# Out projection of a head pair as seven block products of a 2 by 2 scheme, summed in four PSUM banks, on one Trainium2 core

## The reference

```
q = layernorm(x) @ Wq; k, v = ctx @ Wk, ctx @ Wv
attn = softmax(q k^T / sqrt(128)) per head           (256 x 256)
x = x + concat_heads(attn @ v) @ Wo                  (2048 -> 512)
h = layernorm(x); top-4 of 32 experts from sigmoid(h @ gate_w.T) + bias, 2 of 4 groups, capacity 1024
out = x + sum of the chosen experts' silu(h w1) * (h w3) @ w2, weighted
        + silu(h @ shared_gate) * (h @ shared_up) @ shared_down
```

## Time and profile before

| | |
|---|---|
| median of 3 runs | 1640.73 us (1638.84 to 1643.18) |
| profiled execution, its own time | 1646.64 us |
| profiled execution, span | 1644.9 us |
| TensorE (PE) busy | 1605.2 us, 98% |
| VectorE (DVE) busy | 1215.0 us, 74% |
| ScalarE (ACT) busy | 844.8 us, 51% |
| GpSimdE (POOL) busy | 793.6 us, 48% |

### The profile page before, as it was taken

The page is one execution under the profiler, slowest core; times in us unless marked ns, Lnnn a source line. Parts: engine busy times, 40 slices in busy tenths (PEclk is TensorE's granted clock), DMA queues, the critical chain, the costliest instruction groups (busy, mean ns, idle before and its releaser), DMA issues. The chain is left out here.

```text
span 1644.9 us, 35029 instructions
## 1 busy us (share of the span) xinstructions
PE 1605.2 (98%) x12199; PEld 1147.0 (70%) x12199; DVE 1215.0 (74%) x3524; ACT 844.8 (51%) x2094; POOL 793.6 (48%) x1088
## 2 busy tenths in 40 slices
PE   8999999999999999999999999999999999999995
PEld 5667677777777777777777677777777666666663
DVE  7988787777778787787778787877766266776762
ACT  6764444454454454454545454454433266666662
POOL 3443646455564646464554646464345423433422
PEclk9999999999999999999999999999999999999998
DMA  8765444364555445445445444544476578988834
GB/s 261 179 155 110 105 97 111 73 116 79 116 98 115 112 85 110 91 111 97 118 98 111 103 104 105 97 104 91 92 243 199 112 237 225 265 238 219 232 40 55
DMA packets 399662, 218.28 MB, mean 133 GB/s; under 512 B 348400, under 2 KB 356592, under 8 KB 399488
## 3 DMA queue, kind: packets, MB, share of 16 engines
q1 hardware_dynamic: 383024, 189.71, 46.6%
...
q10 hardware_dynamic: 560, 1.05, 0.2%
...
## 5 line engine op out<-in xcount | busy, mean ns | idle before, releaser
L957 ACT ACTIVATE arena<-arena,neg_max 128x256 f32<-128x256 f32 x512 | 253.7, 496 | 377.9 <-DVE neg_max L1260 306.2
L704 POOL TENSOR_SCALAR arena<-arena,prob_scale 128x256 f16<-128x256 f32 x384 | 184.4, 497 | 474.9 <-DVE prob_scale L1269 451.7
L1629 PE MATMUL ps_query<-xn_both,arena 128*128 128x256 f16 x1024 | 279.1, 273 | 0.7 <-DMA xn_both<-xn_half 0.7
L1631 PE MATMUL ps_query<-xn_both,arena 128*128 128x256 f16 x1024 | 279.1, 273 | 0.0
L1630 PE MATMUL ps_query<-xn_both,arena 128*128 128x256 f16 x1024 | 279.1, 273 | 0.0
L1260 DVE CUSTOM_DVE_ANT_0 arena<-ps_score,mask_add 128x256 f32<-128x256 f32 x512 | 186.2, 419 | 78.2 <-PE ps_score L1631 78.2
L1275 DVE SCALAR_TENSOR_TENSOR arena<-arena,prob_scale 128x256 f16<-128x256 f32 x384 | 236.8, 665 | 6.1 <-POOL arena L704 6.1
L1629 PE MATMUL ps_out<-arena,o_t 128*128 128x512 f16 x512 | 194.2, 379 | 1.8 <-DVE o_t L1280 1.7
L1630 PE MATMUL ps_out<-arena,o_t 128*128 128x512 f16 x512 | 194.0, 379 | 0.0
L1631 PE MATMUL ps_out<-arena,o_t 128*128 128x512 f16 x512 | 194.0, 379 | 0.0
L1280 DVE SCALAR_TENSOR_TENSOR o_t<-ps_head,o_t 128x512 f16<-128x512 f32 x128 | 88.3, 690 | 108.6 <-ACT o_t L970 107.8
...
## 6 DMA issues: line engine op xcount, KB each, us to landing
arena<-w SPq DMA_DIRECT2D x96, 512.0 KB, 6.0
...
x_in<-x SPq DMA_DIRECT2D x15, 512.0 KB, 3.9
...
xn_rows<-xn_half SPq DMA_DIRECT2D x15, 512.0 KB
x2t_kept<-xn_both SPq DMA_DIRECT2D x12, 512.0 KB, 2.9
...
weight_in<-wq SPq DMA_DIRECT2D x8, 512.0 KB, 5.3
```

The lines of the kernel that those rows point to most:

```text
L704: pool.tensor_scalar(p_rows[:, c, 0, :], probs[:, c, :], prob_scale[:, c:c + 1], 1.0, ALU.mult, ALU.mult).then_inc(norm_hi, 1)
L957: act.activation(probs[:, c, :], probs[:, c, :], ACT.Exp, bias=neg_max[:, c:c + 1], scale=-1.0, accum_out=prob_sum[:, c:c + 1]).then_inc(e ...
L1629: pe.matmul(dst, a.hi, b.hi, start=start and n == 0, stop=False)
L1631: m = pe.matmul(dst, a.lo, b.hi, start=False, stop=stop and n == len(pairs) - 1)
```

## The change

**Project.** A pair's attended heads form a matrix of 2 by 2 blocks (tokens by heads, 128 each), its output weights one of 2 by 2 blocks (heads by 256 columns). `project(i)` becomes seven products of a sum of blocks on the left and one on the right, each 3 matmuls of 256 columns: 21 in all. They land in the halves of four banks (`ps_sum`: `ps_out0`, `ps_out1`, `ps_head`, `ps_fill0`) and are summed there over a batch; the four output blocks are formed from the banks once a batch, by DVE, in six steps of 512 elements (`residual_first`, `residual_rest`) in place of two. It runs one turn later: `project(i-2)` stands at the end of turn i.

**Left sums.** ACT copies the attended heads to float32 (`head_copy`), GpSimdE forms the sums (`sums`, three tensor_tensor of 256, 128 and 256 elements), ACT writes their `hi` (`sums_high`, 896 elements, at the start of a turn), GpSimdE their `lo` (`sums_low`, 896). `head_low` on DVE goes.

**Right sums.** `combine(g)` on GpSimdE, in turns 1 to 8, forms them from the loaded `wo` of pair g (four tensor_tensor, 512, 256, 256 and 256 elements); `hi` and `lo` of that weight are then 1792 elements instead of 1024. The sums lie in one place, so `combine(g)` waits for `weight_lo` of g - 1.

**Attend** becomes one product set of 512 columns (6 matmuls) into `ps_score1`, after the queries and the key. **Probabilities:** three `hi` on ACT, the fourth on DVE; all four `lo` on DVE; GpSimdE has none. **Exponentials** stand in two halves round the filler's part on ACT. All fillers use `ps_fill1`; values of the next batch stand at j = 1, 3, 4, 6, the gate at 5, the rank at the end of 7. Records run in four parts of two, one batch later.

**Shared FFN.** Its weights are split in turns 11 to 22 in 12 chunks, stored to DRAM and loaded again in the last batch. Its pieces start with 36 in front of the experts, and two beside each of experts 0 to 29; the order of batches in it is (2, 14, 3, 15, ...). The end of the loop on TensorE is attend(127), project(126), two pieces, project(127), four pieces, the last transposes, a piece, the gate, four pieces, the rank, the rest.

```diff
-LATE = (2, 3, 14, 15, 0, 1) + tuple(range(4, 14))
-KEPT = len(LATE) - 4
+LATE = (2, 14, 3, 15, 0, 1) + tuple(range(4, 14))
+IN_PLACE = (0, 1, 3)
...
-EARLY = 32
+EARLY = 36
...
-NOT_BY_POOL = (10, 11, 14, 15, 16)
+NOT_BY_POOL = (14, 15, 16, 17)
...
+LEFT, RIGHT, HALF = 7, 7, D // 2
+BANK_PRODUCTS = (((0, 4), (3, 5)), ((4, 0), (5, 3)), ((6, 6), (2, 2)), ((1, 1),))
+BANKS = len(BANK_PRODUCTS)
+FFN_CHUNKS = 3 * KD
+FFN_FROM = 11
...
+        ps_sum = [ps_out[0], ps_out[1], ps_head, ps_fill[0]]
+        ps_heads = ps_score[1]
...
+        jobs = [by_columns("wk", wk_s, wk, KC, 0, 512, 0), wq_job(0, 1),
+                by_columns("wv", wv_s, wv, KC, 0, 512, 2), wq_job(1, 3),
+                wq_job(2, 0), wq_job(3, 1), by_columns("wv", wv_s, wv, KC, 1, 512, 2), out_rows_job(0, 0),
+                wq_job(4, 1), by_columns("wk", wk_s, wk, KC, 1, 512, 2), out_rows_job(1, 0),
+                wq_job(5, 1), out_rows_job(2, 2), wq_job(6, 0), out_rows_job(3, 1), wq_job(7, 2), out_rows_job(4, 0),
+                out_rows_job(5, 1), out_rows_job(6, 2), out_rows_job(7, 0),
+                ("gate", gate_s, rows_of(gate_t), KD, E, 1)]
         JOBS = len(jobs)
...
+            def combine(g):
+                n = prepared["wo", g] - 1
+                w = weight_at(n)[:, :].rearrange("p (m c) -> p m c", m=4)
+                y = sums_y[:, 0:3 * HALF].rearrange("p (m c) -> p m c", m=3)
+                pool.wait_ge(in_weight[jobs[n][5]], 16 * (same_buffer(n).index(n) + 1))
+                pool.wait_ge(weight_lo, prepared["wo", g - 1] if g else 4)
+                pool.tensor_tensor(y[:, 0:2, :], w[:, 0:4:2, :], w[:, 1:4:2, :], ALU.add).then_inc(*own.up())
+                pool.tensor_tensor(y[:, 2, :], w[:, 0, :], w[:, 3, :], ALU.add).then_inc(*own.up())
+                pool.wait_ge(*own.now())
+                pool.tensor_tensor(w[:, 2, :], w[:, 2, :], w[:, 0, :], ALU.subtract).then_inc(*own.up())
+                pool.tensor_tensor(w[:, 1, :], w[:, 1, :], w[:, 3, :], ALU.subtract).then_inc(combined, 1)
...
+            def sums(i):
+                pool.wait_ge(head_copied, i + 1)
+                pool.tensor_tensor(o_full[:, 4:6, :], o_full[:, 0:2, :], o_full[:, 2:4, :], ALU.add).then_inc(*own.up())
+                pool.tensor_tensor(o_full[:, 6, :], o_full[:, 1, :], o_full[:, 2, :], ALU.add).then_inc(*own.up())
+                pool.wait_ge(*own.now())
+                pool.tensor_tensor(o_full[:, 0:4:3, :], o_full[:, 0:4:3, :], o_full[:, 1:3, :], ALU.subtract).then_inc(
+                    summed, 1)
+            def sums_low(i):
+                pool.wait_ge(sum_hi, i + 1)
+                pool.tensor_tensor(l_t.lo, o_full[:, :, :], l_t.hi, ALU.subtract).then_inc(sum_lo, 1)
...
+                if 1 <= i <= KV:
+                    combine(i - 1)
+                if i >= 2:
+                    sums_low(i - 2)
...
+                if is_out(n):
+                    g = jobs[n][0][1]
+                    act.wait_ge(combined, g + 1)
+                    act.activation(wo_s[:, g, 0:4 * HALF].hi, weight_at(n)[:, :], ACT.Copy, scale=W_S)
+                    act.activation(wo_s[:, g, 4 * HALF:RIGHT * HALF].hi, sums_y[:, 0:3 * HALF], ACT.Copy,
...
+            def probs_high(i, cells):
                 act.wait_ge(prob_scaled, i + 1)
-                c = CELLS - 1
-                act.activation(probs[:, c, :], probs[:, c, :], ACT.Copy, scale=prob_scale[:, c:c + 1]).then_inc(
-                    last_scaled, 1)
-            def head_high(i):
+                for c in cells:
+                    if i:
+                        act.wait_ge(turned[c // TB], 16 * i)
...
+            def sums_high(i):
+                act.wait_ge(summed, i + 1)
+                if i:
+                    act.wait_ge(pe_out, BANKS * i)
+                act.activation(l_t.hi, o_full[:, :, :], ACT.Copy, scale=1.0).then_inc(sum_hi, 1)
...
                 b, g = divmod(i, KV)
                 pe.wait_ge(value_lo, 4 * b + 2 * (g // 4) + SB)
+                pe.wait_ge(maxed, CELLS * min(i + 2, TURNS))
                 if i:
-                    pe.wait_ge(head_lo, i)
+                    pe.wait_ge(head_copied, i)
                 for h in range(PAIR):
                     pe.wait_ge(turned[h], 16 * (i + 1))
-                    cells = slice(h * TB, (h + 1) * TB)
-                    m = products(ps_head[:, h * T:(h + 1) * T].rearrange("p (c t) -> p c t", c=TB),
-                                 [(v_s[b % 2][:, s, g * HD:(g + 1) * HD], p_t[s][:, cells, :]) for s in range(SB)])
-                m.then_inc(pe_head, 1)
+                products(ps_heads[:, :].rearrange("p (c t) -> p c t", c=CELLS),
+                         [(v_s[b % 2][:, s, g * HD:(g + 1) * HD], p_t[s]) for s in range(SB)]).then_inc(pe_head, 1)
 
             def project(i):
                 b, g = divmod(i, KV)
-                pe.wait_ge(head_lo, i + 1)
+                pe.wait_ge(sum_lo, i + 1)
                 pe.wait_ge(weight_lo, prepared["wo", g])
-                if g == 0 and b:
-                    pe.wait_ge(x1_done, TB * b)
-                for t in range(TB):
-                    m = products(ps_out[t][:, :], [(o_t[:, h * T + t * P:h * T + (t + 1) * P], wo_s[:, g * PAIR + h, :])
-                                                   for h in range(PAIR)], start=g == 0, stop=g == KV - 1)
-                m.then_inc(pe_out, 1)
+                for n, parts in enumerate(BANK_PRODUCTS):
+                    if g == 0 and b:
+                        pe.wait_ge(out_read, BANKS * (b - 1) + n + 1)
+                    elif g == 0 and n == BANKS - 1:
+                        pe.wait_ge(value_lo, SB)
+                    for m, (left, right) in enumerate(parts):
+                        last = products(ps_sum[n][:, m * HALF:(m + 1) * HALF],
+                                        [(l_t[:, left, :], wo_s[:, g, right * HALF:(right + 1) * HALF])],
+                                        start=g == 0 and m == 0, stop=g == KV - 1, shared=True)
+                    last.then_inc(pe_out, 1)
 
...
-            for i in range(TURNS + 1):
+            for i in range(TURNS):
                 b, j = divmod(i, KV)
                 if i == 0:
-                    filler(("value", 0, 0, 0), ps_fill[1])
-                if i < TURNS:
-                    scores(i)
+                    filler(("value", 0, 0, 0))
+                scores(i)
                 if i == 0:
-                    filler(("value", 0, 0, 1), ps_fill[0])
+                    value(ps_fill[0], 0, 0, 1)
+                filler(fill(b, j))
                 if i + 1 < TURNS:
-                    query(i + 1, 0)
-                if i < TURNS:
-                    filler(first(b, j), ps_fill[1])
+                    for h in range(PAIR):
+                        query(i + 1, h)
+                    key(i + 1)
                 else:
-                    piece(1)
+                    piece(0)
                 if i:
                     attend(i - 1)
-                if i + 1 < TURNS:
-                    query(i + 1, 1)
-                if i < TURNS:
-                    filler(second(b, j), ps_fill[0])
-                if i + 1 < TURNS:
-                    key(i + 1)
-                if i >= TURNS - 1:
-                    piece((i - TURNS + 1) * 2)
-                if i:
-                    project(i - 1)
+                if i == TURNS - 1:
+                    piece(1)
+                if i >= 2:
+                    project(i - 2)
+                filler(rank_of(b, j))
 
             z = B - 1
-            for k in (3, 4, 5):
+            attend(TURNS - 1)
+            project(TURNS - 2)
+            piece(2)
+            piece(3)
+            project(TURNS - 1)
+            for k in range(4, 8):
                 piece(k)
             pe.wait_ge(ident_halved, 1)
-            pe.wait_ge(maxed, CELLS * TURNS)
+            pe.wait_ge(out_read, BANKS * B)
+            pe.wait_ge(head_copied, TURNS)
             for t in range(TB):
                 last_transposed(t)
-            piece(6)
-            pe.wait_ge(*emptied(before["end", 1]))
+            piece(8)
+            pe.wait_ge(*emptied(LAST_HELD))
             gate(ps_fill[1], z)
-            for k in range(7, 11):
+            for k in range(9, 13):
                 piece(k)
             pe.wait_ge(gate_exp, z + 1)
             rank(ps_fill[1], z)
-            for k in range(11, EARLY - 1):
+            for k in range(13, EARLY - 1):
                 piece(k)
             expert_rows(0)
             piece(EARLY - 1)
```

770 lines of the change are left out of this document (431 added, 339 removed).

## The result

The changed kernel takes **1706.8 us** in the median of 4 runs (1704.8 to 1712.5) against 1639.8 (1637.6 to 1643.2): a ratio of 1.041, interval 1.038 to 1.044, so slower by 67 us. The profiled executions differ by 58.1 us in their spans, less than the medians, since that of the kernel before took 5.9 us more than its median and that of the changed kernel 2.0 less.

What follows compares the result with a forecast made beforehand. TensorE, busy 98% of the span, was taken as the bound. Terms -39.9 + 2 + 21.9 + 8 + 0 = -8.0 us, against the median of 1640.7 a forecast of 1633 us, range 1610 to 1655.

Steps and rivals of the forecast that it cites:

- TensorE's work: Project and attend matmuls in every turn: 0.312 us less a turn, times 128, minus 39.9 us.
- Nothing is over a turn, so I cost the loop at zero: Other engines in a steady turn: each fits, so no loop cost; +2 us for splitting shared FFN weights, bounds 0 and 6.
- The ring: Rival in the loop: ACT and GpSimdE wait on each other, 7.8 against 8.16 us; if it binds, 1650 us; chance 0.2.
- Interference: Rival in the start: GpSimdE lengthens DVE's two-input steps by 0.43 us, +9 us, 1642 us; chance 0.2.
- The start: Up to turn 8: serial weight preparation delays project(0) to 49.9 and turn 8 to 110.2; +21.9 us, bounds +8 and +30.
- the 88.3 of the same sum: Start of turn 8 in us from savings and the deferred project alone, before the start's loss is added.
- a serial link of 11.75 us: In the start, one weight's load, combine, ACT's and DVE's steps in series; sets each turn's price up to the eighth.
- The tail: Between last turn and experts: longer chain to late_split(21), covered by 15 pieces instead of seventeen; +8 us, bounds +2 and +12.
- The forecast wait of 9.6 us: In the tail, TensorE waiting at a down piece after the gate for a GpSimdE split, 2.94 us before.
- The end: Four pieces move from beside experts 30 and 31 to the front, 10.4 us each way; 0, bounds -2 and +3.

Runs made afterwards that it cites:

- run 6: Changed kernel with the edits of run 1 and Run 2 together, lo halves of left sums left out: 1642.7 us.
- Run 2: Changed kernel with sums_low on GpSimdE taking 2 of 128 columns of each sum from the second pair on: 1656.7 us.
- run 5: Run 2 with two memsets of the lo halves in front of the short sums_low, as late but reading nothing of SBUF: 1677.3 us.
- run 13: Changed kernel with only the fourth probability tile's hi moved from VectorE to ScalarE: 1685.9 us.
- run 1: Changed kernel with the next batch's values moved to the end of the turn, behind the project: 1698.5 us.
- run 11: Changed kernel with run 1's late values and sums_low split into four steps: 1708.8 us.
- run 9: Changed kernel with run 4's edit, and hi and lo of the right sums on 2 instead of 768 elements from the second pair on: 1694.6 us.
- run 4: Changed kernel with combine's four steps taking 2 columns for g over 0: 1695.3 us.
- run 10: Changed kernel with the FFN pieces in front of the experts back from 36 to 32, two beside every expert again: 1706.4 us.

## Why the prediction was wrong, point by point

The forecast was 1633 us, 1610 to 1655; the time is 1706.8, and the sign is the other.

1. **TensorE's work, -39.9:** held. Turns without a value take 8.17 us (8.16 forecast), and run 6 comes to 71.91 a batch with 71.3 of work.
2. **"Nothing is over a turn, so I cost the loop at zero": this step failed, by some 50 us.** Waits grew by 12.8 us in turns 8 to 23 and by 42.3 in turns 24 to 119, against 2 forecast. Two things were missed. First, I averaged VectorE to 89% and treated the rest as slack, with each step at its duration in the kernel before; GpSimdE's new reading steps lengthened them, from 6.5 to 13.1 us of held time a batch. Run 2 (-50 us for one GpSimdE step, of which run 5 gives back 21 with a write as late) and run 13 (-21 us for 0.35 us a turn) show both halves of that. Second, I read in the change that all fillers now use `ps_fill1` and priced no wait for it. The key stands 2.6 us of queries behind the value in the same bank; run 1 shows that a later place for the value is not enough by itself, with the bank still shared, and run 6 that the bank is the second limit, 0.76 us a batch, once VectorE is on time.
3. **The ring,** my slower rival: in the changed kernel it never bound. It predicted losses in turns without values; they have none, but for 0.5 us at j = 0, where the scores wait. Its sign, slower, was right for another reason. In run 11 the projects do wait for `sum_lo`, 16.1 us in the loop.
4. **Interference,** a rival for the start only, at 0.43 us a step: the mechanism was right, the size and the place were wrong. A hold lasts up to the rest of a 1.9 us step (2099 ns for a step of 468), and it matters in all 128 turns. The one sentence that gave this size was the one of the Trainium skill's page which I set below the row. And the trace of before had the sign of it, had I looked at the ends:

```profile
1145.74 0.75 POOL L710 TENSOR_TENSOR arena<-arena 128x256 f16<-128x256 f32 x1
1145.88 0.90 DVE L1275 SCALAR_TENSOR_TENSOR arena<-arena,prob_scale 128x256 f16<-128x256 f32 x1
```

All 106 of line 1275's steps that start inside a line 710 of GpSimdE and are stretched by it (773 to 896 ns) end 278 to 286 ns after it. So 0.43 us was the rest of a step of at most 0.75 us, and not a size of its own.
5. **The start, +21.9:** the first link was right to 0.8 us (50.68 for 49.9). Against the 88.3 of the same sum turn 8 is 29.6 late, just inside the upper bound of +30. The reason I gave for the later turns, a serial link of 11.75 us, is not borne out: run 9, with run 4's edit in it, took some 4.5 us (an estimate from the rows) out of each link and turn 8 moved by 6.0.
6. **The tail, +8:** +15.0 from turn 127 to the end, all of it in front of the experts. The forecast wait of 9.6 us is 5.3, and it waits for the landing of an addition; the rest are several waits of 0.8 to 2.3 us, most of them for VectorE. 2.2 us of the wait come from the four moved pieces (run 10). No run took the rest of the tail apart, so its split stays open.
7. **The end, 0:** right within its bounds (-2 to +3): run 10 gives 10.4 us behind the front for 10.4 of work in front, and 2.2 in the wait of the tail.

What stays open: 10.6 us of the start; most of the tail; how much of run 5's loss is delay and how much is holding by writes; and why VectorE's and GpSimdE's steps meet more often in run 11.
